# Graph attention scores on Trainium2: z and one-hots made for pairs of groups, node terms copied by ScalarE and turned for eight groups at once

## The reference, cut to what matters

```
hr_src = h_r[:, src];  hr_dst = h_r[:, dst];  diff = hr_dst - hr_src
score = s_src + s_dst + einsum('hed,hd->he', diff, a_dif) \
      + einsum('hed,hd->he', abs(diff), a_abs) + einsum('hed,hd->he', hr_src * hr_dst, a_prd)
alpha = leaky_relu(score, negative_slope=0.2)
m  = segment_max(alpha.T, src);  ex = exp(alpha.T - m[src])
att = ex / segment_sum(ex, src)[src]
out = segment_sum(att * h_e[:, dst], src)
```

## Time and profile before

| | |
|---|---|
| median of the runs | 3220.21 us |
| the profiled execution | 3229.66 us, its span 3227.9 us |
| PE matmul busy | 81% of the span |
| DVE busy | 71% |
| POOL busy | 48% |
| ACT busy | 22% |
| TensorE's granted clock, mean | 0.914 |
| memory traffic | 150 GB/s over the span |

### The profile page before, as it was taken

How to read it: one execution, slowest core, us unless ns; L and a number is a source line. 1 busy time by engine, 2 the same in 40 slices (tenths; PEclk the granted TensorE clock), 3 DMA queues, 4 the chain that set the end, 5 groups by cost and what they waited for, 6 DMA issues and landing times. The chain is left out here.

```text
span 3227.9 us, 51758 instructions
## 1 busy us (share of the span) xinstructions
PE 2604.2 (81%) x16298; PEld 1661.5 (51%) x16298; DVE 2295.9 (71%) x4733; ACT 697.2 (22%) x1316; POOL 1545.2 (48%) x1568
## 2 busy tenths in 40 slices
PE   2499987799999999999990377878787777777898
PEld 2265653577777767776760244444444444446443
DVE  3577833699999989999999667667677676775222
ACT  1133320233333333333330100000000000004321
POOL 0223311466666666555650256556566565541244
PEclk9699998899999999999995588898888888889899
DMA  4022222877777777777773255555555555554443
GB/s 128 7 62 63 63 92 90 166 191 191 191 192 192 192 190 195 194 194 193 192 176 139 70 162 168 167 163 170 170 170 168 165 168 166 167 155 138 139 128 96
DMA packets 190342, 485.76 MB, mean 150 GB/s; under 512 B 47902, under 2 KB 77934, under 8 KB 189318
## 3 DMA queue, kind: packets, MB, share of 16 engines
q0 software_dynamic: 117200, 384.69, 44.2%
q1 hardware_dynamic: 48324, 71.73, 7.2%
q10 hardware_dynamic: 24562, 26.03, 2.8%
HBM read 437.29 MB, written 46.97 MB: 150 GB/s over the span
## 5 line engine op out<-in xcount | busy, mean ns | idle before, releaser
L1352 PE MATMUL ps_sum<-messages,node_onehot 128*125 128x512 f32 x1344 | 815.5, 701 | 238.8 <-DVE messages L1328 231.6
L1031 POOL DMA_INDIRECT rows_v<-target_rows,edge_dst x672 | 696.6, 1037 | 440.7 <-PE ps_heads L1126 234.9
L1307 POOL DMA_INDIRECT rows_e<-message_rows,edge_dst x672 | 635.2, 945 | 553.5 <-DVE messages L1328 219.8
L1080 DVE SCALAR_TENSOR_TENSOR z<-w_abs,corner 128x256 f32<-128x256 f32 x1344 | 559.8, 478 | 1.3 <-ACT w_abs L1144 1.3
L1099 PE MATMUL ps_u<-edge_space,source_onehot_t 125*128 x4032 | 515.5, 275 | 47.3 <-DVE source_onehot_t L1060 37.1
L1066 DVE TENSOR_TENSOR rows_v<-rows_v,ps_u 128x520 f32<-128x520 f32 x672 | 444.4, 690 | 91.3 <-PE ps_u L1099 51.0
L1144 ACT ACTIVATE w_abs<-ps_w 128x1024 f32<-128x1024 f32 x336 | 343.9, 1024 | 753.4 <-PE ps_w L1114 540.2
L1353 PEld LDWEIGHTS ps_den<-edge_space,node_onehot 128*125 128x125 f32 x1344 | 276.1, 205 | 373.9 <-issue 373.9
L1338 DVE TENSOR_TENSOR edge_space<-ps_sum,edge_space 125x512 f32 x336 | 231.2, 688 | 327.7 <-remote 201.9
L1099 PEld LDWEIGHTS ps_u<-edge_space,source_onehot_t 125*128 125x128 bf16 x4032 | 385.8, 97 | 119.3 <-issue 56.0
L1328 DVE TENSOR_TENSOR messages<-rows_e,ps_beside 128x1024 f32<-128x1024 f32 x336 | 406.8, 1211 | 6.6 <-DMA rows_e<-message_rows,edge_dst 6.3
(11 more groups left out here) (402 smaller groups left out, 2449.0 us busy)
## 6 DMA issues: line engine op xcount, KB each, us to landing
scores<-score SPq DMA_DIRECT2D x1344, 8.0 KB
edge_ids<-local_ids ACTq DMA_DIRECT2D x112, 187.5 KB
edge_space<-in_L_ffn_w_dram SPq DMA_DIRECT2D x24, 512.0 KB, 4.1
rows_v<-target_rows,edge_dst POOLq DMA_INDIRECT x672
rows_e<-message_rows,edge_dst POOLq DMA_INDIRECT x672
source_parts<-edge_space SPq DMA_DIRECT2D x20, 380.9 KB
edge_space<-source_parts SPq DMA_DIRECT2D x4, 1904.3 KB
edge_space<-scores SPq DMA_DIRECT2D x2, 2688.0 KB, 24.1
```

What stands on the lines that cost most here:

```text
L1031: nc.gpsimd.indirect_dma_start(rows[q][:, j, :], None, tab_v, bass.IndirectOffsetOnAxis(ap=edge["dst"][:, tile:tile + 1], axis=0)).then_in ...
L1080: ins = v.scalar_tensor_tensor(z[h][:, c, :], w_abs[h][:, c, :], corner[:, c:c + 1], w_abs[h][:, c, :], ALU.subtract, ALU.mult)
L1307: nc.gpsimd.indirect_dma_start(rows[q][:, j, :], None, tab_e, bass.IndirectOffsetOnAxis(ap=edge["dst"][:, tile:tile + 1], axis=0)).then_in ...
L1352: nc.tensor.matmul(ps_sum[h][:, :], onehot[h][:, j, :], messages[h][:, j, :], start=j == 0, stop=j == GROUP - 1)
```

## The change

- `multiply`: z is made in place in `w_abs`, for two groups at once: two of the four chunks when the even group's turn comes, two when the odd group's does, each of 512 columns. `w_abs` has four pair buffers (eight groups) in place of three `w_abs` and three `z`.
- `locate`: the one-hot of two groups in one instruction of 512 columns, in two pair buffers.
- `add_heads`: the node terms' two matmuls go. Instead ACT copies each group's node terms (128 x 2 x 8) into a buffer `edge_terms` (`collect`, a new step behind the magnitudes), and after every eighth group (SET = 8) PE transposes that buffer once, 128x128, into free columns of `ps_heads`. The score copy of such a group is 384 columns wide, and SP stores the turned terms with 8 more DMAs into a fifth part of `scores`.
- `softmax_weights`: a fifth part is loaded, after the first addition, into the buffer of the second part, and added.
- The gathered buffer comes free when the terms are copied. The ids are fetched four groups at a time (three sets). Steps stand further behind: z 5, head sums 7, score copy 13.

```diff
-    ID_GROUPS, ID_SETS = 3, 4
+    ID_GROUPS, ID_SETS = 4, 3
+    PAIRS, MARKS, SET = 4, 2, P // (GROUP * HEADS)
...
-        onehot_t = sbs("source_onehot_t", [L, GROUP, P], BF16)
-        w, w_abs = rows, sbs("w_abs", [P, KF, GE])
-        z = sbs("z", [P, KF, GE])
-        score = sbs("score", [P, GE])
+        onehot_t = [sb(f"source_onehot_t{m}", [L, 2, GROUP, P], BF16) for m in range(MARKS)]
+        w, w_abs = rows, [sb(f"w_abs{m}", [P, KF, 2, GE]) for m in range(PAIRS)]
+        z = w_abs
+        terms = [sb(f"edge_terms{m}", [P, HEADS, SET * GROUP]) for m in range(2)]
+        score = sbs("score", [P, GE + P])
...
@@ SP, stores
+                if ends_set(n):
+                    for h in range(HEADS):
+                        sp.dma_start(scores[KF * HEADS + h, (n + 1 - SET) * GE:(n + 1) * GE].rearrange("(t e) -> t e", e=P),
+                                     score[n % BUFS][h * SET * GROUP:(h + 1) * SET * GROUP, GE:GE + P]).then_inc(score_out[n % BUFS], 16)
@@ POOL, gather
-                    pool.wait_ge(summed, n - RING + 1)
+                    pool.wait_ge(collected, n - RING + 1)
@@ DVE
             def locate(n, q, turn):
-                at_least(dve, ids_in[q // ID_GROUPS], turn * 16 + 16)
-                at_least(dve, expanded, (n - BUFS + 1) * GROUP)
-                x = q % ID_GROUPS * GE
-                v.tensor_scalar(onehot_t[q % BUFS]..., ids[q // ID_GROUPS][:, x:x + GE], col[0:L, 0:1], None, ALU.is_equal).then_inc(located, 1)
+                if n % 2 == 0:
+                    at_least(dve, ids_in[q // ID_GROUPS], turn * 16 + 16)
+                    at_least(dve, expanded, (n - 2 * MARKS + 2) * GROUP)
+                    x = q % ID_GROUPS * GE
+                    v.tensor_scalar(onehot_t[n // 2 % MARKS]..., ids[q // ID_GROUPS][:, x:x + 2 * GE], col[0:L, 0:1], None, ALU.is_equal).then_inc(located, 1)
...
             def multiply(n, q, turn):
-                h = q % BUFS
-                at_least(dve, abs_set, n + 1)
-                at_least(dve, summed, n - BUFS + 1)
-                for c in range(KF):
-                    ins = v.scalar_tensor_tensor(z[h][:, c, :], w_abs[h][:, c, :], corner[:, c:c + 1], w_abs[h][:, c, :], ALU.subtract, ALU.mult)
+                h = n // 2 % PAIRS
+                at_least(dve, abs_set, n // 2 * 2 + 2)
+                for c in range(n % 2 * KF // 2, (n % 2 + 1) * KF // 2):
+                    both = w_abs[h][:, c, :, :].rearrange("p i e -> p (i e)")
+                    ins = v.scalar_tensor_tensor(both, both, corner[:, c:c + 1], both, ALU.subtract, ALU.mult)
                 ins.then_inc(z_set, 1)
-            in_turns(TURNS, ((2, differ_first), (2, differ_second), (4, multiply), (0, locate)), TURN)
+            in_turns(TURNS, ((2, differ_first), (2, differ_second), (5, multiply), (0, locate)), TURN)
@@ PE
             def add_heads(n, q, turn):
-                at_least(pe, z_set, n + 1)
+                at_least(pe, z_set, n // 2 * 2 + 2)
                 at_least(pe, score_kept, n - 1)
...
-                for j in range(GROUP):
-                    strip = ps_heads[q % 2][j * STRIP:j * STRIP + HEADS, j * P:(j + 1) * P]
-                    ins = nc.tensor.matmul(strip, w[q % RING][:, j, F:EW], ident[:, :], start=False, stop=True, skip_group_check=True)
+                if ends_set(n):
+                    at_least(pe, collected, n + 1)
+                    ins = nc.tensor.transpose(ps_heads[q % 2][:, GE:GE + P], terms[n // SET % 2][:, :, :].rearrange("p h t -> p (h t)"), ident[:, :])
                 ins.then_inc(summed, 1)
-            in_turns(TURNS, ((2, expand_first), (2, expand_second), (5, add_heads), (3, transpose)), TURN)
+            in_turns(TURNS, ((2, expand_first), (2, expand_second), (7, add_heads), (3, transpose)), TURN)
@@ ACT
             def magnitudes(n, q, turn):
-                at_least(act, z_set, n - BUFS + 1)
-                sc.activation(w_abs[h][:, :, :], ps_w[:, :, :], ACT.Abs).then_inc(abs_set, 1)
+                at_least(act, summed, (n // 2 - PAIRS + 1) * 2)
+                sc.activation(w_abs[h][:, :, n % 2, :], ps_w[:, :, :], ACT.Abs).then_inc(abs_set, 1)
+            def collect(n, q, turn):
+                at_least(act, summed, (n // SET - 1) * SET)
+                t = n % SET * GROUP
+                sc.copy(terms[n // SET % 2][:, :, t:t + GROUP].rearrange("p h t -> p t h"), w[q % RING][:, :, F:EW]).then_inc(collected, 1)
             def keep_scores(n, q, turn):
+                width = GE + P if ends_set(n) else GE
                 at_least(act, summed, n + 1)
...
-            in_turns(TURNS, ((9, magnitudes), (0, fetch_ids), (11, keep_scores)), TURN)
+            in_turns(TURNS, ((9, magnitudes), (9, collect), (0, fetch_ids), (13, keep_scores)), TURN)
@@ softmax_weights, SP
+            sp.wait_ge(first_added, 1)
+            sp.dma_start(score_parts[1], scores[KF * HEADS:(KF + 1) * HEADS, :].rearrange("h (c x) -> (h c) x", c=CHUNKS)).then_inc(scores_in[KF], 16)
@@ softmax_weights, DVE
+                if k == 1:
+                    dve.sem_inc(first_added, 1)
+            dve.wait_ge(scores_in[KF], 16)
+            link(v.tensor_tensor(score_parts[0], score_parts[0], score_parts[1], ALU.add))
```

More of the change, by code:

```diff
@@ L955, in score_edges @@
     BUFS, RING, TURN = 3, 6, 12
-    ID_GROUPS, ID_SETS = 3, 4
+    ID_GROUPS, ID_SETS = 4, 3
+    PAIRS, MARKS, SET = 4, 2, P // (GROUP * HEADS)
+    assert GROUPS % SET == 0 and SET % 2 == 0
     TURNS = GROUPS // TURN
@@ L997, in score_edges, with ends_set, stores_before @@
         vectors_in, iota_set, vectors_set, link_s = sem("vectors_in"), sem("head_iota_set"), sem("vectors_set"), sem("score_link")
+        def ends_set(n):
+            return n % SET == SET - 1
+        def stores_before(n):
+            return sum(KF + (HEADS if ends_set(m) else 0) for m in range(n % BUFS, n, BUFS))
         block = ctx.enter_context(nc.Block())
@@ L1016, in _ @@
                     sp.dma_start(scores[c * HEADS:(c + 1) * HEADS, n * GE:(n + 1) * GE],
-                                 score[n % BUFS][c * STRIP:c * STRIP + HEADS, :]).then_inc(score_out[n % BUFS], 16)
+                                 score[n % BUFS][c * STRIP:c * STRIP + HEADS, 0:GE]).then_inc(score_out[n % BUFS], 16)
+                if ends_set(n):
+                    for h in range(HEADS):
+                        sp.dma_start(scores[KF * HEADS + h, (n + 1 - SET) * GE:(n + 1) * GE].rearrange("(t e) -> t e", e=P),
+                                     score[n % BUFS][h * SET * GROUP:(h + 1) * SET * GROUP, GE:GE + P]).then_inc(score_out[n % BUFS], 16)
             for h in range(BUFS):
-                sp.wait_ge(score_out[h], GROUPS // BUFS * (16 * KF))
+                sp.wait_ge(score_out[h], 16 * stores_before(GROUPS + h))
         @block.gpsimd
@@ L1098, in expand @@
                         rows_of_part = parts[:, DS(b, 1), part, half * HALF:(half + 1) * HALF].rearrange("p o c -> p (o c)")
-                        ins = nc.tensor.matmul(ps_u[j][:, half, 0:HALF], onehot_t[q % BUFS][:, j, :], rows_of_part, start=part == 0, stop=part == PARTS - 1)
+                        ins = nc.tensor.matmul(ps_u[j][:, half, 0:HALF], onehot_t[n // 2 % MARKS][:, n % 2, j, :], rows_of_part, start=part == 0, stop=part == PARTS - 1)
                 ins.then_inc(expanded, 1)
@@ L1136, in fetch_ids @@
                 if q % ID_GROUPS == 0:
-                    at_least(act, located, n - TURN + ID_GROUPS)
+                    at_least(act, located, (n - TURN + ID_GROUPS) // 2)
                     act.dma_start(ids[q // ID_GROUPS][:, :], local_ids[DS(n, ID_GROUPS), :].rearrange("g x -> (g x)").partition_broadcast(L)).then_inc(ids_in[q // ID_GROUPS], 16)
             def magnitudes(n, q, turn):
-                h = q % BUFS
+                h = n // 2 % PAIRS
                 at_least(act, turned, n + 1)
-                at_least(act, z_set, n - BUFS + 1)
-                sc.activation(w_abs[h][:, :, :], ps_w[:, :, :], ACT.Abs).then_inc(abs_set, 1)
+                at_least(act, summed, (n // 2 - PAIRS + 1) * 2)
[4 more added lines that the diff above has]
+                sc.copy(terms[n // SET % 2][:, :, t:t + GROUP].rearrange("p h t -> p t h"), w[q % RING][:, :, F:EW]).then_inc(collected, 1)
             def keep_scores(n, q, turn):
+                width = GE + P if ends_set(n) else GE
                 at_least(act, summed, n + 1)
-                at_least(act, score_out[q % BUFS], n // BUFS * (16 * KF))
-                sc.copy(score[q % BUFS][:, :], ps_heads[q % 2][:, 0:GE]).then_inc(score_kept, 1)
-            in_turns(TURNS, ((9, magnitudes), (0, fetch_ids), (11, keep_scores)), TURN)
+                at_least(act, score_out[n % BUFS], 16 * stores_before(n))
+                sc.copy(score[n % BUFS][:, 0:width], ps_heads[q % 2][:, 0:width]).then_inc(score_kept, 1)
+            in_turns(TURNS, ((9, magnitudes), (9, collect), (0, fetch_ids), (13, keep_scores)), TURN)
```

(5 more changed lines are left out.)

9 lines of the change are left out of this document (5 added, 4 removed).

## The result

On the chip of the first measurement the changed kernel takes 3393.95 us (3387.18 to 3396.03), the kernel before 3218.39: ratio 1.0545 [1.0523, 1.0567], **slower by 5.5%** where 3% faster was forecast. On another chip the same two kernels stood at 2912.09 and 2962.44: 0.9829 [0.9813, 0.9846], **1.7% faster**. (The record gives the first chip no number: three of the four runs behind 3218.39 are those given with the time before, and the fourth took 3208.93.) I call the first kind quiet chips, the others chips with late reports, for a reason the traces give.

What follows compares the result with a forecast made beforehand. PE and DVE were both taken as close to their limits in scoring, at 3.303 us a group. 3220.2 - 105 (period 2.99) + 10 (paid once) = 3125 us, range 3075 to 3170.

Steps and rivals of the forecast that it cites:

- PE's floor, 2.83: PE, scoring: node terms' matmuls go (-0.32), a transpose per eight groups comes (0.015 a group); 3.13 to 2.83 us.
- z and one-hots: DVE, scoring: two 512-wide z instructions save 0.27 us a group, paired one-hots 0.06; floor 3.00 to 2.67 us.
- ScalarE and the stores: ACT's added 128x16 copy, 0.24 us, and SP's stores, 1.7 us a group on average, are both hidden.
- POOL: POOL in scoring: gather buffer freed earlier, own floor 2.68 us a group, below PE's 2.83; costed at nothing.
- rival C: POOL becomes the bound as denser DVE work stretches gathers to 1.45 us: 3.51 us a group, 3300 us; chance 0.04.
- Paid once, +10: Scoring stage's end +4 us, fifth softmax addition 5.8 us with its reload covered; sum +10 us.
- The period: Scoring group time: 3.303 to 2.99 us, between 3.00 from PE and 2.97 from DVE; saves 105 us.
- With PE's present loss: Scoring: PE's 0.17 us a group over its floor stays, 2.83 + 0.17 = 3.00; DVE's 0.30 likewise, 2.97.
- the handshake: Waits between PE and DVE in scoring, taken to cause losses of 0.17 and 0.30 us a group over their floors.
- more lead, no work less: Gather's buffer comes free at ACT's copy, some two turns minus the gain earlier; costed at nothing.
- Rival B: PE-DVE waits become the bound, 0.45 us on average: 3.12 us a group, 3170 us; chance 0.17.
- At 0.63 in each, 3.30: DVE's 0.63 us wait for ps_u in every group: 3.30 us, nothing gained, +10 would show; chance 0.02.

Runs made afterwards that it cites:

- the half that unloaded PE: Only the node terms' part of the change, z and one-hots per single group as before, against the kernel before on a quiet chip: 2926.43 us, ratio 0.9882.
- the half that unloaded DVE: Only z and one-hots for two groups, node terms staying on PE, against the kernel before on a quiet chip: 2963.96 us, ratio 1.0013.
- the gather behind the heads: Changed kernel, gather also waiting for head sums of group n - 8: 2945.77 us quiet (0.9949 of before); 3258.05 with late reports (before 3173.57).

## Why the prediction was wrong

By its own steps:

- **PE's floor, 2.83: too low by 0.11.** It is 2.94. The removed matmuls had begun 0.45 us behind the heads; with transposes behind them instead the heads take 0.57. So the node terms gave back 0.20 a group and not 0.32. The transpose for eight groups costs 0.17, not 0.12.
- **z and one-hots: right.** 0.665 us an instruction of 512 columns against 0.661, the one-hot pair 0.27 against 0.26, DVE's floor 2.68 against 2.67. The fixed time of an instruction is 0.13 us at both widths, and the saving came as the row had it. The Trainium skill, VectorE: DVE Perf Modes, section on the TRN2 errata, has 58 cycles of fixed time, 0.06 us as an estimate at its 0.96 GHz; that would have been wrong for this saving. The same section of the Trainium skill says that in a measured copy the fixed term was about 150 cycles, which is 0.16 us, as an estimate, and nearer to it.
- **ScalarE and the stores: right.** The copy of 128x16 takes 0.21 us and is hidden.
- **POOL: right, rival C false.** The gather's mean went from 1037 to 991 ns, and it is 1030 on the quiet chip, far from 1.33 us.
- **Paid once, +10: +12.3.** 5.8 for the addition, as said, with its reload hidden. The stage's end is 6.4 later, not 4: from the last magnitudes' start to the first load of the softmax it is 1877.36 - 1864.16 = 13.2 us, where it was 6.8.
- **The period: the step that failed.** "With PE's present loss" and "with DVE's" carried 0.17 and 0.30 us over as if they belonged to the kernel. They didn't. On a quiet chip the same kernel runs at 3.148 (3.129 once its first 21 groups are through), PE at its floor of 3.13: the loss I called the handshake was that chip's late reports, and it is no constant of the kernel. In the changed kernel the transposes' reports came 288 us late in all instead of 109, and the loss over the floor became 3.786 - 2.94 = 0.85 us, not 0.17. The likely reason is that the change moved POOL's gather to another place in the turn, which I had costed at nothing ("more lead, no work less"); this last link is argued, and not shown.

Rival B named the right wait, DVE's for ps_u, and gave it 0.45 us a group; it was 3.786 - 2.68 = 1.11 over DVE's floor. "At 0.63 in each, 3.30" was where I stopped counting. The row of 0.63 was one of 144 such waits, and 45 were longer, 16 of them over 1.5 us; I hadn't looked for them. On quiet chips the period came out near by luck, from two errors of opposite sign, a floor 0.11 too low and a loss 0.17 too high: 2.931 against 2.99. The saving there was 1.7% where 3% was forecast, for the kernel before had next to no loss to start from (3.148 over a floor of 3.13).

## What to carry to other kernels

Where an engine's floor and its measured period differ, find out what each lost microsecond is before carrying it over: list the waits by length, and if their lengths scatter while the work is the same in each turn, something outside the schedule may be behind them, which a change of order can make dearer or cheaper. Measure on more than one chip. When a resource's release is moved (here the gather's), write down where in the turn the released work will now run, even if its engine has time to spare. Take off the engine that is full first: the half that unloaded PE brought 0.158 of the 0.217 us, and the half that unloaded DVE showed only once the other was there.

## What was unexpected of the hardware

- One kernel, two kinds of chips: 2957 to 2962 us on six, 3174 and 3218 on others. The messages stage, the same code in all kernels, takes 2.511 us a group on the first kind and 3.145 on the other (before), 3.085 with the gather behind the heads.
- PE's semaphore reports arriving up to 3.5 us late, several at a time, with PE idle and nothing in its rows to show it, while DVE's come within 0.012 us. They do so in the two stages full of gathers and not in those behind them.
- Heads of 128x256 in four strips: 0.45 us when short matmuls into the strips follow, 0.57 when 128x128 transposes do.
- DVE's z over 512 columns in place costs 0.665 us, so 0.13 us of fixed time an instruction, at 256 and 512 columns alike.
- Replacing 672 gathers of 128 rows by plain loads of as many rows changed the time by about 0.1% on a quiet chip.
